# The feed-forward net of a graph layer on plain float32 factors in place of split ones

## The reference

```python
weights = (jnp.einsum('bsd,do->bso', x, wr) + br)[..., 0]
_, idx = jax.lax.top_k(weights, k)
sel_idx = idx[:, :kk]
sel = jnp.take_along_axis(x, sel_idx[:, :, None], axis=1)
h = jax.nn.gelu(jnp.einsum('bkd,dh->bkh', sel, w1) + b1)     # 256 -> 1024
y = jnp.einsum('bkh,hd->bkd', h, w2) + b2                    # 1024 -> 256
y = y * w_sel[..., None]
processed = jnp.zeros_like(x).at[batch_idx, sel_idx].set(y)
return processed + x
```

## Time and profile before

| | us |
|---|---|
| median of 3 runs | 2729.84 (2728.61 to 2730.43) |
| profiled execution, time | 2730.12 |
| profiled execution, span | 2728.4 |
| TensorE busy | 2256.7 (83%) |
| VectorE busy | 1356.8 (50%) |
| ScalarE busy | 952.2 (35%) |
| POOL busy | 1617.5 (59%) |
| mean granted clock of TensorE | 0.909 |

### The profile page before, as it was taken

How to read it: one execution, slowest core, us unless ns; L and a number is a source line. 1 busy time by engine, 2 the same in 40 slices (tenths; PEclk the granted TensorE clock), 3 DMA queues, 4 the chain that set the end, 5 groups by cost and what they waited for, 6 DMA issues and landing times.

```text
span 2728.4 us, 51169 instructions
## 1 busy us (share of the span) xinstructions
PE 2256.7 (83%) x13608; PEld 1868.5 (68%) x13609; DVE 1356.8 (50%) x3596; ACT 952.2 (35%) x2178; POOL 1617.5 (59%) x1719
## 2 busy tenths in 40 slices
PE   1399999978898888889888888888888996169998
PEld 0287777766677666667666676666667775169998
DVE  8644444443333344344444444444445888854444
ACT  8433333322222222222222222222224997035454
POOL 3577777777777777777777777777770000023332
PEclk6699999989888888998989899999989998579999
DMA  9766666654444444444444444444443997012221
GB/s 316 220 197 187 179 185 184 184 183 132 145 139 140 136 143 140 139 144 135 140 139 143 136 143 137 143 140 140 138 134 128 311 308 253 0 44 65 66 68 41
DMA packets 229947, 412.27 MB, mean 151 GB/s; under 512 B 38193, under 2 KB 129715, under 8 KB 229886
## 3 DMA queue, kind: packets, MB, share of 16 engines
q0 software_dynamic: 81296, 224.22, 28.8%
q1 hardware_dynamic: 147774, 186.59, 20.3%
q10 hardware_dynamic: 816, 0.79, 0.1%
HBM read 315.13 MB, written 96.32 MB: 151 GB/s over the span
## 4 chain that ended last, share of the span: by engine, by line
PE 34%; POOL 31%; issue 14%; DVE 12%; DMA 4%; DVEq 2%; ACT 1%; POOLq 0%; SPq 0%
POOL gath_raw L621 31%; PE ps L1539 10%; PE ps L1413 6%; PE ps L1336 4%; PE ps L1338 3%; DMA gath_raw<-xtab,srcI 3%; PE ps L1381 3%; PE ps L1423 2%; PE ps L1455 1%; DVEq L411 1%; DVE work L939 1%; DVE onehot L936 1%; DVE onehot L923 1%; DVE agg L975 1%; DVE stats L837 1%
## 5 line engine op out<-in xcount | busy, mean ns | idle before, releaser
L621 POOL DMA_INDIRECT gath_raw<-xtab,srcI x1563 | 1477.9, 946 | 476.4 <-issue 461.8
L1336 PE MATMUL ps<-gath_raw,onehot 128*128 128x256 f16 x1956 | 489.3, 286 | 203.5 <-DMA gath_raw<-xtab,srcI 89.7
L1338 PE MATMUL ps<-gath_raw,onehot 128*128 128x257 f16 x1956 | 490.5, 287 | 0.0
L767 DVE SCALAR_TENSOR_TENSOR onehot<-ps,blkbase,dstF 128x512 f32 x489 | 352.2, 746 | 243.6 <-issue 216.3
L1413 PE MATMUL ps<-work,w_s 128*128 128x256 f32 x1568 | 409.2, 419 | 1.0
L1336 PEld LDWEIGHTS ps<-gath_raw,onehot 128*128 x1956 | 198.1, 101 | 298.6 <-issue 267.8
L1413 PEld LDWEIGHTS ps<-work,w_s 128*128 128x128 f32 x1568 | 323.2, 212 | 51.7 <-issue 0.5
L777 DVE TENSOR_TENSOR agg<-agg,ps x98 | 41.4, 423 | 522.0 <-PE ps L1338 521.8
L1539 PE MATMUL ps<-split_raw 128*128 128x256 f32 x2376 | 293.4, 285 | 1.7 <-DVE split_raw L1053 1.5
L1539 PEld LDWEIGHTS ps<-split_raw 128*128 128x128 f32 x2376 | 288.5, 193 | 2.4 <-issue 1.9
L633 POOL COPY agg<-agg 128x2 int32 (+2 forms) x25 | 6.8, 273 | 389.3 <-DVE agg L1042 351.2
(11 more groups left out here) (197 smaller groups left out, 3230.0 us busy)
## 6 DMA issues: line engine op xcount, KB each, us to landing
work<-x_in SPq DMA_DIRECT2D x98, 256.0 KB, 3.1
ff_d<-work SPq DMA_DIRECT2D x49, 512.0 KB, 2.8
gath_raw<-xtab,srcI POOLq DMA_INDIRECT x1563
agg<-x_in SPq DMA_DIRECT2D x14, 896.0 KB, 7.3
xtab<-gath_raw SPq DMA_DIRECT2D x14, 896.0 KB, 4.9
xt_d<-work SPq DMA_DIRECT2D x49, 256.0 KB, 4.2
q_d<-work SPq DMA_DIRECT2D x49, 256.0 KB, 2.4
work<-q_d SPq DMA_DIRECT2D x49, 256.0 KB, 3.4
```

What stands on the lines that cost most here:

```text
L621: e.indirect_dma_start(out=gath[:, TPG * s + t, 0:2 * D], out_offset=None, in_=xtab[:, :], in_offset=bass.IndirectOffsetOnAxis(ap=srcI[:, ...
L767: v.scalar_tensor_tensor(out=onehots[:, ds(p % OHN * TPG, TPG), :], in0=ps[:, columns:columns + 1, 0:P].to_broadcast(shape), scalar=blkbas ...
L1336: t.matmul(ps[:, ds(BG + k % 2, 1), 0:D], oh, gath[:, r, 0:D], start=False, stop=False, skip_group_check=True)
L1338: last = t.matmul(ps[:, ds(BG + k % 2, 1), 0:AGW], oh, gath[:, r, D:2 * D + 1], start=False, stop=q == TPG - 1, skip_group_check=True)
```

## The change

The feed-forward net multiplies the float32 tiles as they are. A product that was three calls of `matmul` on float32r tiles becomes one on float32 tiles: 32 calls in a step in place of 96. The copies and subtractions that made the high and low parts go, for the weights, the rows and the hidden values, and so do their semaphores. ScalarE's copy of the transposed rows (`f_xs`) now releases TensorE by itself, and gelu releases the output products. The tile `agg` is now a tensor of its own at the place of `split_raw`. The other stages are as they were.

```diff
@@ -5,7 +5,6 @@
 
 f32 = mybir.dt.float32
 f16 = mybir.dt.float16
-f32r = mybir.dt.float32r
 i32 = mybir.dt.int32
 ALU = mybir.AluOpType
 ACT = mybir.ActivationFunctionType
@@ -134,8 +133,6 @@
             return v.rearrange("p a b -> p (a b)")
 
 
-        with nc.sbuf_tensor("agg", [P, NBLK, AGW], f32) as agg:
-            pass
 
         def ln_sent(eng, n):
 
@@ -143,7 +140,7 @@
                 if len(range(k, n, LNT)):
                     eng.wait_ge(ln_out[k], 16 * len(range(k, n, LNT)))
 
-        split_raw = sb("split_raw", [P, NBLK, AGW], f32r)
+        agg = sb("agg", [P, NBLK, AGW])
         gath_raw = sb("gath_raw", [P, RING * TPG * GROW // 2])
         gath = gath_raw[:, :].bitcast(f16).rearrange("p (s c) -> p s c", c=GROW)
         wq_s = sb("wq_s", [P, 2, D])
@@ -311,12 +308,7 @@
         fstage = [sem(f"fstage{i}") for i in range(FSLOTS)]
         f_in = [sem(f"f_in{i}") for i in range(FSLOTS)]
         f_T_ps = sem("f_T_ps")
-        f_wh = sem("f_wh")
-        f_wl = sem("f_wl")
-        f_xT_h = sem("f_xT_h")
         f_xT = sem("f_xT")
-        f_g = sem("f_g")
-        f_hh = sem("f_hh")
         f_h_ps = sem("f_h_ps")
         f_h = sem("f_h")
         f_y_ps = sem("f_y_ps")
@@ -369,7 +361,6 @@
         raw_c, raw_n = (work[0:1, a:a + NG - 1] for a in (6480, 5136))
 
         pool2 = agg[:, :, :].rearrange("p b c -> p (b c)")
-        pool2r = split_raw[:, :, :].rearrange("p b c -> p (b c)")
         s_gt, s_eq, s_rank, s_colf = (pool2[:, 128 * k:128 * k + NBLK] for k in range(4))
         s_pos, s_q = (pool2[:, 128 * k:128 * k + NBLK].bitcast(i32) for k in (5, 6))
         s_sum = [pool2[:, 128 * k:128 * k + NBLK] for k in (7, 8)]
@@ -389,20 +380,12 @@
         fstg = [pool2[:, 1760 + 2 * k:1762 + 2 * k].bitcast(i32) for k in range(FSLOTS)]
         frow = [part(pool2, 2048 + 1024 * k, (2, 2 * D)) for k in range(FSLOTS)]
 
-        f_xh = [part(pool2r, 5120 + 512 * k, (2, SB)) for k in range(FSLOTS)]
-        f_xl = [part(pool2r, 14848 + 512 * k, (2, SB)) for k in range(FSLOTS)]
+        f_xs = [part(pool2, 5120 + 512 * k, (2, SB)) for k in range(FSLOTS)]
         fo = [part(pool2, 6656 + 512 * k, (2, D)) for k in range(FSLOTS)]
         fh = part(pool2, 8192, (HF // P, SB))
         f_junk = part(pool2, 10240, (2, D))
         fw1_s = part(pool2, 10752, (2, HF))
         fw2_s = part(pool2, 10752 + 2 * HF, (HF // P, D))
-        fh_h = part(pool2r, 16384, (HF // P, SB))
-        fw1_h = part(pool2r, 20480, (2, HF))
-        fw2_h = part(pool2r, 20480 + 2 * HF, (HF // P, D))
-
-        fh_l = part(pool2r, 8192, (HF // P, SB))
-        fw1_l = part(pool2r, 10752, (2, HF))
-        fw2_l = part(pool2r, 10752 + 2 * HF, (HF // P, D))
 
         def seg_values(eng, etype, g0, n):
 
@@ -1042,26 +1025,8 @@
             v.tensor_tensor(sel_idx, s_sum[0][:, 0:NSEL], ps[:, BD, 0:NSEL], ALU.add).then_inc(s_idx, 1)
 
 
-            e.wait_ge(f_wh, 2)
-            v.tensor_tensor(fw1_l, fw1_s, fw1_h.bitcast(f32), ALU.subtract).then_inc(f_wl, 1)
-            v.tensor_tensor(fw2_l, fw2_s, fw2_h.bitcast(f32), ALU.subtract).then_inc(f_wl, 1)
-
-            def f_low_x(i, s):
-                e.wait_ge(f_xT_h, i + 1)
-                if past(i, FSLOTS):
-                    e.wait_ge(f_h_ps, 4 * (i - FSLOTS + 1))
-                v.tensor_tensor(f_xl[s], bank(BA), f_xh[s].bitcast(f32), ALU.subtract).then_inc(f_xT, 1)
-
-            f_low_x(0, 0)
-
             def f_body(i, s, j):
                 n = 1 if isinstance(i, int) and i == FSTEPS - 1 else 2
-                for h in range(4):
-                    e.wait_ge(f_hh, 4 * i + h + 1)
-                    c = slice(2 * h, 2 * h + 2)
-                    v.tensor_tensor(fh_l[:, c, :], fh[:, c, :], fh_h[:, c, :].bitcast(f32), ALU.subtract).then_inc(f_h, 1)
-                if not (isinstance(i, int) and i == FSTEPS - 1):
-                    f_low_x(i + 1, (s + 1) % FSLOTS)
                 e.wait_ge(f_in[s], 32 * j + 16 * n)
                 if past(i, 1):
                     e.wait_ge(f_o, i)
@@ -1256,21 +1221,13 @@
             steps(e, g_body, NSUP, 2, 3)
 
 
-            e.wait_ge(ffw_in, 32)
-            a.activation(fw1_h, fw1_s, ACT.Copy).then_inc(f_wh, 1)
-            a.activation(fw2_h, fw2_s, ACT.Copy).then_inc(f_wh, 1)
-
             def f_copy(i, s):
                 e.wait_ge(f_T_ps, i + 1)
                 if past(i, FSLOTS):
                     e.wait_ge(f_h_ps, 4 * (i - FSLOTS + 1))
-                a.activation(f_xh[s], bank(BA), ACT.Copy).then_inc(f_xT_h, 1)
+                a.activation(f_xs[s], bank(BA), ACT.Copy).then_inc(f_xT, 1)
 
             f_copy(0, 0)
-
-            def f_high(i, h):
-                e.wait_ge(f_g, 4 * i + h + 1)
-                a.activation(fh_h[:, 2 * h:2 * h + 2, :], fh[:, 2 * h:2 * h + 2, :], ACT.Copy).then_inc(f_hh, 1)
 
             def f_body(i, s, j):
                 for h in range(4):
@@ -1280,8 +1237,7 @@
                     for c in (2 * h, 2 * h + 1):
                         last = a.activation(fh[:, c, :], bank(BB + h)[:, c % 2, :], ACT.Gelu_apprx_tanh,
                                             bias=fb1_s[:, c:c + 1])
-                    last.then_inc(f_g, 1)
-                    f_high(i, h)
+                    last.then_inc(f_h, 1)
                 if not (isinstance(i, int) and i == FSTEPS - 1):
                     f_copy(i + 1, (s + 1) % FSLOTS)
             steps(e, f_body, FSTEPS, FSLOTS, 2)
@@ -1533,26 +1489,17 @@
                 last.then_inc(f_T_ps, 1)
             f_T(0, 0, 0, 2)
 
-            def split_products(to, left, right, start, stop):
-
-                for k, (l, r) in enumerate(((0, 0), (0, 1), (1, 0))):
-                    last = t.matmul(to, left[l], right[r], start=start and k == 0, stop=stop and k == 2)
-                return last
-
-            e.wait_ge(f_wl, 2)
-
             def f_body(i, s, j):
                 end = isinstance(i, int) and i == FSTEPS - 1
                 n = 1 if end else 2
                 e.wait_ge(f_xT, i + 1)
                 for o_ in range(HF // P):
                     if past(i, 1) and o_ % 2 == 0:
-                        e.wait_ge(f_g, 4 * i - 3 + o_ // 2)
+                        e.wait_ge(f_h, 4 * i - 3 + o_ // 2)
                     for c in range(2):
                         cols = slice(o_ * P, (o_ + 1) * P)
-                        last = split_products(bank(BB + o_ // 2)[:, o_ % 2, :],
-                                              [w[:, c, cols] for w in (fw1_h, fw1_l)],
-                                              [x_[s][:, c, :] for x_ in (f_xh, f_xl)], c == 0, c == 1)
+                        last = t.matmul(bank(BB + o_ // 2)[:, o_ % 2, :], fw1_s[:, c, cols], f_xs[s][:, c, :],
+                                        start=c == 0, stop=c == 1)
                     if o_ % 2:
                         last.then_inc(f_h_ps, 1)
                 if not end:
@@ -1564,8 +1511,8 @@
                     for c in range(HF // P):
                         if u == 0 and c % 2 == 0:
                             e.wait_ge(f_h, 4 * i + c // 2 + 1)
-                        last = split_products(bank(BF)[:, u, :], [h_[:, c, u * P:(u + 1) * P] for h_ in (fh_h, fh_l)],
-                                              [w[:, c, :] for w in (fw2_h, fw2_l)], c == 0, c == HF // P - 1)
+                        last = t.matmul(bank(BF)[:, u, :], fh[:, c, u * P:(u + 1) * P], fw2_s[:, c, :],
+                                        start=c == 0, stop=c == HF // P - 1)
                 last.then_inc(f_y_ps, 1)
             steps(e, f_body, FSTEPS, FSLOTS, 2)
```

## The result

| | before | after |
|---|---|---|
| median | 2729.9 us | 2783.73 us (2781.95 to 2784.41) |
| span of the profiled execution | 2728.4 us | 2781.7 us |
| granted clock, mean | 0.909 | 0.912 |

The changed kernel takes 1.0197 times as long, 95% interval 1.0179 to 1.0215. Forecast were 2785.7 us and slower; it came 2 us lower. Beside the experiments the kernel before had medians of 2730.2 to 2731.1 us. `all_waits` and `f16_two_banks` met a condition in which every kernel, the one before too (3220.8 us), took some 490 us longer, all of it ahead of the net, so both were run once more.

The account below looks back on a forecast made before the run. TensorE was taken to bound the net from its first product on. Terms 55.0 + 5.0 + 0 - 0.7 - 3.2 - 0.2 = +55.9 us on 2729.84 gave 2785.7 us, range 2779 to 2796, slower at 0.93.

Parts of the forecast that it names:

- part 1: Net's 792 products on TensorE: a plain one takes two records, 0.4317 us against 0.3622 for three split ones; +55.0 us.
- part 2: Edges around a step's four transposes: 0.56 us in place of 0.35, 24 times, +5.0 us.
- part 3: Cold start of the net at granted clock 0.50: plain products lose as much as split ones; 0, within half a microsecond.
- part 4: Splitting work removed: nothing in steady steps; at the start -0.7 (first split) and -3.2 us (POOL freed), last step -0.2.
- What is late next: Output products waiting for gelu: six plain products (2.6 us) with the transposes cover it, so nothing comes late.
- Loads setting the pace: Rival: weight loads price TensorE's products, so 64 in place of 96 give 96 us less, 2630 us; chance 0.04.
- A gap or a lower clock in the steps: Rival: a pause or clock fall each step, 2.2 us a step, +53 more, 2838 us; 1 us gap 2810; chance 0.05.
- One record in place of two: Rival: plain products built in one record at a reduced one's price, some 170 us less; chance 0.01.
- The check by the Trainium skill: Page estimate for part 1: 0.427 us a plain product against 0.320 for three single passes, making it +84 us.

Follow-up runs that it names:

- all_waits: Kernel before with all copies, subtractions and waits kept, only TensorE's calls made plain float32: 3277.73 us in the slow condition, 2787.8 us when run again.
- f16_two_banks: Kernel before with float16 parts, weight subtractions behind POOL's first gathers, output products reordered into two PSUM banks: 3193.16 us in the slow condition, 2701.93 us rerun.
- hybrid: Changed kernel's plain float32 for the 16 hidden products of a step only, output products split in three as in the kernel before: 2757.56 us, ratio 1.0101.
- keep_wsub: Changed kernel with two unused VectorE subtractions of the weights' size put back at the start: 2786.59 us, ratio 1.0205 to the kernel before.
- late_low: Kernel before with VectorE's two weight subtractions moved behind POOL's first gathers: 2727.45 us, ratio 0.9989.
- plain_halfcols: Changed kernel with each hidden product made as two calls of 128 moving columns in place of one of 256: 2790.14 us, ratio 1.0216 to the kernel before.
- f16: Kernel before with high and low parts in float16 in place of float32r, still three calls a product: 2713.97 us, ratio 0.9939.

## Why the prediction was right, point by point

The spans differ by 53.3 us. The end of the net on TensorE, first before (L1531 are the last transposes), then after:

```profile
2700.64 0.38 PE L1531 MATMUL ps<-ident,agg 128*128 128x128 f32 x2
2700.78 14.11 PE L1539 MATMUL ps<-split_raw 128*128 128x256 f32 x114
2715.05 0.98 PE L1539 MATMUL ps<-split_raw 128*128 128x256 f32 x6 [0.16 <-DVE split_raw L1062]
```
```profile
2751.69 0.38 PE L1487 MATMUL ps<-ident,agg 128*128 128x128 f32 x2
```

From the second step's transposes to the last ones there are 23 steps: 2700.64 - 2425.99 = 274.65 us before and 2751.69 - 2423.88 = 327.81 after. Of the 53.16 us between them, 23 x 32 x 0.0695 = 51.15 are products and 2.0 edges. With the first step and the last the parts of the sum are:

| term | predicted | measured |
|---|---|---|
| part 1, 792 products | +55.0 | +55.0 |
| part 2, edges at transposes | +5.0 | +2.0 |
| part 3, cold start | 0 | +0.4 |
| part 4, start of the net | -3.9 | -3.95 |
| part 4, last step | -0.2 | -0.5 |
| stages ahead of the net | 0 | +0.3 |
| sum | +55.9 | +53.3 |

**Part 1** held. The pace read from 12 records of another stage, 0.2158 us, is that of the net's 1584 records, and `hybrid` shows it beside the split one in a single step. 792 x (0.4316 - 0.3621) = 55.0.

**Part 2** is the mis-sized term. The step predicted from it was 14.37 us, and it is 14.25. Predicted were 0.56 us for the transposes with their edge; measured 0.44 (2723.18 to 2723.62), with the records ahead at full pace. The place that I read, 2163.74 to 2165.16 in the earlier trace rows, holds a wait that the net doesn't have. These are the transposes ahead of it and behind it, in the kernel before:

```profile
2160.66 0.66 PE L1321 MATMUL ps<-ident,work 128*128 128x128 f32 x4 [0.22 <-ACT work L1220]
...
2169.27 0.66 PE L1321 MATMUL ps<-ident,work 128*128 128x128 f32 x4 [0.49 <-ACT work L1220]
```

There the transposes wait for rows that ScalarE writes (L1220). At 2164.67 no wait is shown for them, but their weight load waited 0.30 us for the same L1220, which ended at 2164.62. From 2105 to 2246 us every group of transposes in this stage comes at least 0.03 us late and then takes 0.48 to 0.50 us. Around 2101 us, in the same stage, nothing is waited for:

```profile
2100.95 1.03 PE L1488 MATMUL ps<-wlT,work 128*128 128x256 f32 x4
2101.81 0.60 PE L1321 MATMUL ps<-ident,work 128*128 128x128 f32 x4
2102.25 1.03 PE L1488 MATMUL ps<-wrT,w_s 128*128 128x256 f32 x4
```

Here the four records take 0.86 us and the transposes 0.44, which is what the net has after the change, where the transposes find their rows ready. So the step that was off took an edge with a late operand for one without; 24 x 0.12 us is the 3 us of the table. Why late transposes also take 0.05 us longer themselves is not shown. The smaller misses add up to 0.4 us the other way and the medians differ by 53.8 us, 0.5 more than the spans, so the forecast was off by 2 us in the end and not by 3.

**Part 3.** The first 32 plain records took 2423.88 - 2414.37 = 9.51 us where warm ones take 6.91: 2.6 us lost, against 2.16 before. The granted clock was 0.50 at the start in both. 0.4 us were within the half microsecond allowed.

**Part 4.** TensorE's first product starts 3.67 us earlier (2414.37 for 2418.04) though all ahead of it is 0.28 us later; that gives 3.95. The wait before the first transpose is 6.5 us (9.6 before), and 0.69 us instead of 1.50 before the first product. The cause, VectorE's two-input subtractions holding POOL up, was argued then and is shown now, by `keep_wsub` and `late_low` from either side. The copy in the kernel before ends 0.05 us after its subtraction, but the gather 0.85 us after, and not just after it, as the prediction had it. The rule of the Trainium skill that the prediction named for it (SBUF — State Buffer, "SBUF: two separate sides") agrees with all three traces. In the last step of the kernel before, 114 split records took 14.27 us (2700.78 to 2715.05) for 114 x 0.1207 = 13.76: the stops at splits there were 0.5 us in all, of which the list of waits showed 0.16.

**What is late next:** nothing, as forecast. The only wait of TensorE after the first transpose is the 0.7 us before its first product; `all_waits_again` shows that even the whole splitting work would fit under the longer step.

**The rivals.** Loads setting the pace: ruled out by `plain_halfcols`. A gap or a lower clock in the steps: not there, clock 1.00 and no idle time. One record in place of two: there are 1584. The check by the Trainium skill (FP8 and Floating Point Precision, "TensorE Precision Notes") would have given an estimated +84 us; the estimate from its four passes fits the plain product (0.432 us measured, 0.427 estimated), but three split calls cost 0.362 us and not 0.320. The run `f16` puts the same calls at 3 x 0.109 = 0.327: it is the float32r call that is dearer than its columns.

## What to carry to other kernels

Count TensorE's records, not its calls, and take the time of one from the distance between starts, at a place where nothing is waited for: here one plain float32 product (two records, 0.432 us) is 19% dearer than three float32r calls (0.362 us) and 32% dearer than three float16 ones (0.327 us). Work on other engines that hides under TensorE brings nothing when it is taken out, but it sets how far TensorE can be sped up: 96 calls at 0.109 us already met the splitting work, and 64 calls ran into it for good. Where a stage starts cold, look at what VectorE does while POOL prepares the first transfer; moving two subtractions gave some 3 us at no cost.

## What the runs showed of the hardware

- At granted clock 1.00, records of 128 columns start 0.112 us apart in float32 and in float32r; with 256 columns a plain float32 record takes 0.2158 us, a float32r call 0.1207 us and a float16 call 0.109 us.
- While VectorE subtracts two tiles of SBUF (2.28 us), a copy of POOL takes 2.18 us in place of 0.18, and the issue of a gather 2.16 to 2.65 us in place of 0.96; the gather ends 0.84 or 0.85 us after the subtraction.
- Four transposes take 0.44 us ahead of plain float32 or float16 products and 0.36 us ahead of float32r ones. Where they come late for waiting for ScalarE, in the output stage, they take 0.48 to 0.50 us. Why these differ wasn't tried.
